# Attention with relative positions on one core: scores and value products merged in twos, PSUM ring cut from five banks to three

## The reference

```python
qkv = x @ qkv_w.T + qkv_b                     # x is the normed input; q and v also get x @ la.T @ lb.T
attn = einsum('bqd,bkd->bqk', q * hd ** -0.5, k)
rel_h = einsum('bhwc,hkc->bhwk', r_q, Rh)     # r_q is q as a 14 x 14 grid
rel_w = einsum('bhwc,wkc->bhwk', r_q, Rw)
attn = softmax(attn + rel_h[..., :, None] + rel_w[..., None, :])
out = (attn @ v) @ proj_w.T + proj_b          # output: input + out
```

## Time and profile before

| | us |
|---|---|
| median of 3 runs (3370.44 to 3375.27) | 3372.74 |
| the profiled execution, its own time | 3373.03 |
| its span | 3371.3 |
| TensorE matmuls busy | 3297.2 (98%) |
| DVE busy | 2528.2 (75%) |
| ACT busy | 2098.2 (62%) |
| share of the last chain of work on TensorE | 94% |
| mean granted TensorE clock | 0.991 |

### The profile page before, as it was taken

The page is one execution under the profiler, slowest core; times in us unless marked ns, Lnnn a source line. Parts: engine busy times, 40 slices in busy tenths (PEclk is TensorE's granted clock), DMA queues, the critical chain, the costliest instruction groups (busy, mean ns, idle before and its releaser), DMA issues.

```text
span 3371.3 us, 80148 instructions
## 1 busy us (share of the span) xinstructions
PE 3297.2 (98%) x31984; PEld 2130.7 (63%) x31984; DVE 2528.2 (75%) x5970; ACT 2098.2 (62%) x5651; POOL 35.8 (1%) x65
## 2 busy tenths in 40 slices
PE   7689999999999999999999999999999999999998
PEld 4456666666666666666666666666666666666665
DVE  7577777777777777777777777777777777777764
ACT  2466666666666666666666666666666666666664
POOL 0000000000000000000000000000000000000000
PEclk9799999999999999999999999999999999999999
DMA  3145664555555556565555555555565555565554
GB/s 128 42 96 109 120 122 103 115 113 112 118 121 107 113 112 114 116 121 107 110 116 113 112 123 118 101 117 111 110 127 120 100 118 108 111 126 122 103 106 105
DMA packets 1091412, 376.13 MB, mean 112 GB/s; under 512 B 916696, under 2 KB 1071320, under 8 KB 1091040
## 3 DMA queue, kind: packets, MB, share of 16 engines
q1 hardware_dynamic: 1075206, 333.63, 49.8%
q10 hardware_dynamic: 15834, 37.37, 3.9%
HBM read 86.60 MB, written 38.54 MB: 37 GB/s over the span
## 4 chain that ended last, share of the span: by engine, by line
PE 94%; DVE 2%; ACT 1%; issue 0%; DMA 0%; POOL 0%; SPq 0%; POOLq 0%; DVEq 0%
PE ring L556 51%; PE ring L623 17%; PE score L599 9%; PE o_ps L613 7%; PE ring L578 3%; PE ring L637 3%; PE ring L629 3%; ACT prob L682 1%; PE ring L642 0%; PE ring L563 0%; DVE split L789 0%; DVE row_max L769 0%; DVE rel_sb L762 0%; DVE split L781 0%; DVE rel_sb L756 0%
## 5 line engine op out<-in xcount | busy, mean ns | idle before, releaser
L556 PE MATMUL ring<-xn_hi,w_hi 128*128 128x392 f16 x3456 | 1143.2, 331 | 4.8 <-DVE xn_lo L839 4.6
L556 PE MATMUL ring<-xn_lo,w_hi 128*128 128x392 f16 x3456 | 1139.8, 330 | 0.0
L556 PE MATMUL ring<-xn_hi,w_lo 128*128 128x392 f16 x3456 | 1139.3, 330 | 0.5 <-issue 0.5
L682 ACT ACTIVATE prob<-score,neg_max,exp_scale 98x196 f32<-98x196 f32 x1536 | 769.8, 511 | 252.9 <-DVE neg_max L773 245.4
L769 DVE TENSOR_REDUCE row_max<-score 98x4 f32<-98x784 f32 x384 | 373.3, 972 | 273.2 <-PE score L599 272.1
L789 DVE SCALAR_TENSOR_TENSOR split<-prob,row_inv,split 98x196 f16<-98x196 f32 x1536 | 545.0, 417 | 7.8
L556 PEld LDWEIGHTS ring<-xn_hi,w_hi 128*128 128x128 f16 x3456 | 342.3, 99 | 260.7 <-issue 7.7
L556 PEld LDWEIGHTS ring<-xn_hi,w_lo 128*128 128x128 f16 x3456 | 338.8, 98 | 237.9 <-issue 3.6
L556 PEld LDWEIGHTS ring<-xn_lo,w_hi 128*128 128x128 f16 x3456 | 338.9, 98 | 208.3 <-issue 1.9
L623 PE MATMUL ring<-o_hi,w_hi 128*128 128x392 f16 x1152 | 380.2, 330 | 1.4 <-DVE o_lo L798 1.4
L623 PE MATMUL ring<-o_lo,w_hi 128*128 128x392 f16 x1152 | 379.8, 330 | 0.0
(11 more groups left out here) (118 smaller groups left out, 4896.7 us busy)
## 6 DMA issues: line engine op xcount, KB each, us to landing
y_sb<-in_x SPq DMA_DIRECT2D x192, 196.0 KB
out<-y_sb SPq DMA_DIRECT2D x192, 196.0 KB
x_sb<-in_x ACTq DMA_DIRECT2D x31, 1176.0 KB
rel_q<-rel_sb SPq DMA_DIRECT2D x128, 122.5 KB, 2.4
stage<-in_L_conv_qkv_w SPq DMA_DIRECT2D x3, 2304.0 KB, 15.4
turned<-split SPq DMA_TRANSPOSE x384, 4.2
rel_q<-rel_sb SPq DMA_DIRECT2D x128, 24.5 KB, 1.9
v_tok<-v_split SPq DMA_TRANSPOSE x192, 3.4
```

The lines of the kernel that those rows point to most:

```text
L556: last = T.matmul(ring[:, bank, 0:NT], w[:, c, 128 * j:128 * j + 128], xx[:, par, c, :], start=(c == 0 and part == 0), stop=(c == CT - 1 a ...
L682: last = A.activation(prob[:, head, half, :], score[0:HALF, head, TOK * half:TOK * half + TOK], ACT.Exp, bias=neg_max[:, k % 2, i:i + 1], ...
```

## The change

Each head pair's two scoring slots are issued in a row, and its two value slots too. For this the score tensor has four banks (image x head) and the ring three; prob has a half per image, S of slot k waits only for the exps of slot k - 2, and the four orders are rewritten. y_sb has two slots in place of three. The R tables keep one set of 32 columns per row in place of two.

```diff
-BANKS = 5
+BANKS = 3
-YS = 3
+YS = 2
 PE_ORDER = (
-    each("S", 0, 0) + each("P", 1, 10) + each("Z", 2, 5) + each("X", -1, 3, 4, 5) + each("V", 0, 0)
-    + each("S", 0, 1) + each("P", 1, 11) + each("K", 0, 1) + each("Y", 1, 0) + each("G", -1, 0)
-    + each("S", 0, 2) + each("P", 0, 0) + each("G", -1, 1) + each("V", 0, 1) + each("Y", 1, 1) + each("Z", 1, 0)
-    + each("S", 0, 3) + each("P", 0, 1) + each("K", 0, 2) + each("Y", 1, 2) + each("Z", 1, 1)
...
-    + each("S", 0, 9) + each("P", 0, 7) + each("R", -1, 0) + each("K", 0, 5) + each("R", -1, 1) + each("Y", 1, 3)
-    + each("S", 0, 10) + each("P", 0, 8) + each("R", -1, 2, 3, 4) + each("V", 0, 5) + each("Y", 1, 4) + each("Z", 1, 3)
-    + each("S", 0, 11) + each("P", 0, 9) + each("K", -1, 0) + each("X", -2, 0, 1, 2) + each("Y", 1, 5) + each("Z", 1, 4))
+    each("S", 0, 0, 1) + each("P", 1, 10, 11) + each("Z", 2, 5) + each("X", -1, 3, 4, 5) + each("V", 0, 0)
+    + each("K", 0, 1) + each("Y", 1, 0) + each("G", -1, 0)
+    + each("S", 0, 2, 3) + each("P", 0, 0, 1) + each("G", -1, 1) + each("V", 0, 1) + each("Y", 1, 1) + each("Z", 1, 0)
+    + each("K", 0, 2) + each("Y", 1, 2) + each("Z", 1, 1)
+    + each("S", 0, 4, 5) + each("P", 0, 2, 3) + each("V", 0, 2) + each("Z", 1, 2) + each("Q", -1, 0) + each("K", 0, 3)
+    + each("Q", -1, 1)
+    + each("S", 0, 6, 7) + each("P", 0, 4, 5) + each("V", 0, 3) + each("Q", -1, 2) + each("K", 0, 4) + each("Q", -1, 3, 4)
+    + each("S", 0, 8, 9) + each("P", 0, 6, 7) + each("Q", -1, 5) + each("V", 0, 4) + each("R", -1, 0) + each("K", 0, 5)
+    + each("R", -1, 1) + each("Y", 1, 3)
+    + each("S", 0, 10, 11) + each("P", 0, 8, 9) + each("R", -1, 2) + each("V", 0, 5) + each("R", -1, 3) + each("Y", 1, 4)
+    + each("R", -1, 4) + each("Z", 1, 3) + each("K", -1, 0) + each("X", -2, 0, 1) + each("Y", 1, 5) + each("X", -2, 2)
+    + each("Z", 1, 4))
 ACT_ORDER = (
...
+    each("Y", 2, 5) + each("N", 0, 0) + each("X", -1, 3) + each("T", 0, 0) + each("P", 1, 11) + each("X", -1, 4)
+    + each("N", 0, 1) + each("X", -1, 5) + each("V", 0, 0) + each("T", 0, 1) + each("K", 0, 1)
+    + each("Y", 1, 0) + soft(2) + each("P", 0, 1) + each("N", 0, 3) + each("V", 0, 1) + each("T", 0, 3)
+    + each("H", -1, 0) + each("Y", 1, 1) + each("K", 0, 2) + each("H", -1, 1)
+    + each("Y", 1, 2) + each("H", -1, 2) + soft(4) + each("P", 0, 3) + each("N", 0, 5) + each("V", 0, 2) + each("T", 0, 5)
...
+    + each("Y", 1, 3) + each("N", 0, 10) + each("R", -1, 2) + each("T", 0, 10) + each("V", 0, 5) + each("P", 0, 9)
+    + each("N", 0, 11) + each("R", -1, 3) + each("T", 0, 11) + each("Y", 1, 4) + each("R", -1, 4) + each("K", -1, 0)
     + each("X", -2, 0, 1, 2))
 DVE_ORDER = (
...
+    each("Z", 2, 4) + each("S", 0, 0, 1) + each("Z", 2, 5) + each("N", 0, 0) + each("X", -1, 3) + each("T", 0, 0)
+    + each("P", 1, 11) + each("N", 0, 1) + each("V", 0, 0) + each("T", 0, 1) + each("K", 0, 1) + each("X", -1, 4, 5)
+    + each("M", -1, 0)
+    + each("G", -1, 0) + each("S", 0, 2, 3) + each("G", -1, 1) + soft(2) + each("P", 0, 1) + each("N", 0, 3)
+    + each("V", 0, 1) + each("T", 0, 3) + each("H", -1, 0) + each("Z", 1, 0) + each("K", 0, 2) + each("H", -1, 1, 2)
+    + each("Z", 1, 1) + each("S", 0, 4, 5) + each("L", -1, 0, 1) + each("N", 0, 4) + each("L", -1, 2) + each("P", 0, 3)
+    + each("T", 0, 4) + each("V", 0, 2) + soft(5) + each("Z", 1, 2) + each("Q", -1, 0) + each("K", 0, 3)
...
+    + each("S", 0, 10, 11) + each("N", 0, 10) + each("R", -1, 2) + each("T", 0, 10) + each("V", 0, 5) + each("P", 0, 9)
+    + each("N", 0, 11) + each("R", -1, 3) + each("T", 0, 11) + each("R", -1, 4) + each("Z", 1, 3) + each("K", -1, 0)
     + each("X", -2, 0, 1, 2))
 SP_ORDER = (
...
+    each("ST", 2, 4) + each("CB", 0, 0) + each("LY", 1, 0) + each("ST", 2, 5) + each("T", 0, 0) + each("VT", 0, 0)
+    + each("T", 0, 1)
...
+    + each("T", 0, 10) + each("VT", 0, 5) + each("T", 0, 11) + each("CA", -1, 0) + each("ST", 1, 3) + each("LY", 1, 5))
...
-        rt_hi = sb(keep, "rt_hi", [128, 2, H, 64], F16)
+        rt_hi = sb(keep, "rt_hi", [128, 2, H, 32], F16)
...
-        prob = S("prob", [HALF, 2, 2, TOK], F32)
+        prob = S("prob", [HALF, 2, 2, 2, TOK], F32)
...
-        score = own.enter_context(nc.psum_tensor("score", [128, 2, 512], F32))
+        score = own.enter_context(nc.psum_tensor("score", [128, 2, 2, 512], F32))
...
-                    wait(sp, y_out[k % YS], 32 * p + 16 * (k // YS))
+                    wait(sp, y_out[k % YS], 16 * (CT // YS) * p + 16 * (k // YS))
...
-                                    last = T.matmul(cols, tab[rows, ax, row, 32 * head:32 * head + 32], mov,
+                                    last = T.matmul(cols, tab[rows, ax, row, :], mov,
...
-                    wait(pe, exps_done, 12 * p + k)
+                    wait(pe, exps_done, 12 * p + k - 1)
...
-                                last = T.matmul(score[0:HALF, head, to], stat[rows, qs], kk[rows, :],
+                                last = T.matmul(score[0:HALF, image, head, to], stat[rows, qs], kk[rows, :],
```

More of the change, by code:

```diff
@@ L76 @@
 ACT_ORDER = (
[L77 to L83, removed]
@@ new lines @@
+    + each("N", 0, 1) + each("X", -1, 5) + each("V", 0, 0) + each("T", 0, 1) + each("K", 0, 1)
+    + each("Y", 1, 0) + soft(2) + each("P", 0, 1) + each("N", 0, 3) + each("V", 0, 1) + each("T", 0, 3)
+    + each("H", -1, 0) + each("Y", 1, 1) + each("K", 0, 2) + each("H", -1, 1)
+    + each("Y", 1, 2) + each("H", -1, 2) + soft(4) + each("P", 0, 3) + each("N", 0, 5) + each("V", 0, 2) + each("T", 0, 5)
+    + each("Q", -1, 0) + each("K", 0, 3)
+    + each("Q", -1, 1) + soft(6) + each("P", 0, 5) + each("N", 0, 7) + each("V", 0, 3) + each("T", 0, 7) + each("Q", -1, 2)
@@ L90 @@
+    + each("LD", -2, 0) + each("K", 0, 4) + each("Q", -1, 3)
+    + each("Q", -1, 4) + soft(8) + each("P", 0, 7) + each("Q", -1, 5) + each("N", 0, 9) + each("V", 0, 4) + each("R", -1, 0)
+    + each("T", 0, 9) + each("K", 0, 5) + each("R", -1, 1)
+    + each("Y", 1, 3) + each("N", 0, 10) + each("R", -1, 2) + each("T", 0, 10) + each("V", 0, 5) + each("P", 0, 9)
+    + each("N", 0, 11) + each("R", -1, 3) + each("T", 0, 11) + each("Y", 1, 4) + each("R", -1, 4) + each("K", -1, 0)
     + each("X", -2, 0, 1, 2))
@@ L93 @@
 DVE_ORDER = (
[L94 to L106, removed]
@@ new lines @@
+    + each("M", -1, 0)
[3 more added lines that the diff above has]
+    + each("T", 0, 4) + each("V", 0, 2) + soft(5) + each("Z", 1, 2) + each("Q", -1, 0) + each("K", 0, 3)
+    + each("S", 0, 6, 7) + each("Q", -1, 1) + each("N", 0, 6) + each("T", 0, 6) + each("P", 0, 5) + each("V", 0, 3)
@@ new lines @@
+    + soft(7) + each("Q", -1, 2) + each("K", 0, 4) + each("Q", -1, 3)
+    + each("S", 0, 8, 9) + each("Q", -1, 4) + soft(8) + each("P", 0, 7) + each("Q", -1, 5) + each("N", 0, 9)
+    + each("V", 0, 4) + each("R", -1, 0) + each("T", 0, 9) + each("K", 0, 5) + each("R", -1, 1)
+    + each("S", 0, 10, 11) + each("N", 0, 10) + each("R", -1, 2) + each("T", 0, 10) + each("V", 0, 5) + each("P", 0, 9)
+    + each("N", 0, 11) + each("R", -1, 3) + each("T", 0, 11) + each("R", -1, 4) + each("Z", 1, 3) + each("K", -1, 0)
@@ L117 @@
 SP_ORDER = (
[L118 to L129, removed]
+    each("ST", 2, 4) + each("CB", 0, 0) + each("LY", 1, 0) + each("ST", 2, 5) + each("T", 0, 0) + each("VT", 0, 0)
+    + each("T", 0, 1)
+    + each("LY", 1, 1) + each("T", 0, 2) + each("VT", 0, 1) + each("T", 0, 3) + each("ST", 1, 0)
+    + each("ST", 1, 1) + each("LY", 1, 2) + each("T", 0, 4) + each("VT", 0, 2) + each("T", 0, 5) + each("ST", 1, 2)
+    + each("LY", 1, 3)
+    + each("T", 0, 6) + each("VT", 0, 3) + each("T", 0, 7) + each("LY", 1, 4)
+    + each("T", 0, 8) + each("VT", 0, 4) + each("T", 0, 9)
+    + each("T", 0, 10) + each("VT", 0, 5) + each("T", 0, 11) + each("CA", -1, 0) + each("ST", 1, 3) + each("LY", 1, 5))
 PER_PAIR = {"Q": 6, "K": 6, "V": 6, "R": RCH, "Y": 6, "Z": 6, "X": 6, "G": 2}
@@ L162, in build @@
         w_lo = sb(keep, "w_lo", [128, CT, 4 * C], F16)
-        rt_hi = sb(keep, "rt_hi", [128, 2, H, 64], F16)
-        rt_lo = sb(keep, "rt_lo", [128, 2, H, 64], F16)
+        rt_hi = sb(keep, "rt_hi", [128, 2, H, 32], F16)
+        rt_lo = sb(keep, "rt_lo", [128, 2, H, 32], F16)
         onehot = sb(keep, "onehot", [128, TOK], F16)
@@ L380, in _ @@
                 for head in range(2):
-                    for at in (32 * head, 32 * head + 16):
+                    for at in (0, 16):
                         rows = slice(64 * head, 64 * head + 64)
@@ L534, in _ @@
                 elif kind == "LY":
-                    wait(sp, y_out[k % YS], 32 * p + 16 * (k // YS))
+                    wait(sp, y_out[k % YS], 16 * (CT // YS) * p + 16 * (k // YS))
                     sp.dma_start(y_sb[:, k % YS], x_rows[p][:, :, 128 * k:128 * k + 128]).then_inc(y_in[k % YS], 16)
             for slot in range(YS):
-                sp.wait_ge(y_out[slot], 16 * 2 * pairs)
+                sp.wait_ge(y_out[slot], 16 * (CT // YS) * pairs)
         @block.tensor
```

(12 more changed lines are left out.)

15 lines of the change are left out of this document (removed).

## The result

The changed kernel takes 3441.2 us (median of 4 runs, 3438.9 to 3442.8) against 3372.2 before: a ratio of 1.020 (95% interval 1.0185 to 1.0221), 69 us slower. The forecast was 3416, range 3375 to 3460, slower with a chance of 0.80.

What follows compares the result with a forecast made beforehand. The prediction took TensorE's work, practically without waits, to bound the kernel. From 3373.0 us it took 71 for merged slots and added 114 for ring waits with three banks: 3416 us, range 3375 to 3460.

Steps and rivals of the forecast that it cites:

- What the change removes: Six merges of scoring and value slots per pair of images save 0.37 us each, 0.10 of it full-tiling return; 71 us.
- What costs nothing: Second score buffer, prob halves, smaller R tables, shorter memsets, moved X2 and two y buffers: all taken as 0.
- The rel copies as next bound: On SP, relative-position copies land late for the next pair's first scores, hidden only by the last group's waits; 0.7 us.
- The walk: Group by group, TensorE waits for both readers of the ring user three places earlier; 3.68 us per pair, 114 us.
- Groups b to f: Second to last merged groups of a pair of images; waits 0.51 in b, 0.54 in c, none d/e, 1.75 and 0.43 in f.
- the 1.75 us at Z3: In the last group, Z3 takes R3's bank and waits 1.75 us for ACT and DVE to read it.
- group a: First merged group of a pair of images, slots 0 and 1; one wait of 0.45 us forecast.
- The 0.45 at V0: In group a, V0 comes three ring places behind X3 and waits 0.45 us for ACT's late copy of it.
- 31 pairs times one value: Waits of 3.68 us counted for 31 pairs of images, since first and last have other neighbours; 114 us.
- The faster one: Rival: readers keep up, mainly at Z3 behind R3, so waits total under 2.2 us per pair; 3324 or 3302 us; chance 0.14.
- The clock: Rival: the granted clock falls behind each 1.75 us wait, adding up to 53 us; 3469 us; chance 0.12.
- The transposes' rival: Slot 1's transposed split lands 1 us late, so P1 waits in every pair; 31 us more, 3447 us; chance 0.10.

Runs made afterwards that it cites:

- Experiments 1: Changed kernel with TensorE's order inside all six merged groups set back to score, value, score, value; 3473.3 us, ratio 1.030 to the kernel before.
- 7: Kernel of experiment 6 with TensorE's order score, value, score, value inside each group; 3387.2 us, ratio 1.003 to the kernel before.
- experiment 4: Changed kernel with three y_sb slots in place of two, orders unchanged; 3437.0 us, ratio 1.019 to the kernel before.
- experiment 3: Changed kernel with ACT and DVE reading R3 before slot 11's softmax and P9, and ACT reading Y4 earlier; 3416.0 us, ratio 1.013 to the kernel before.
- experiment 8: Kernel of experiment 6 with SP issuing transpose T11 ahead of store ST3 and ACT loading the next input later; 3345.7 us, ratio 0.992 to the kernel before.
- experiment 6: Changed kernel with reader orders rewritten against ring waits, Y5 between X0 and X1, three y_sb slots, merge kept; 3351.9 us, ratio 0.993 to the kernel before.
- experiment 2: Kernel before the change with four ring banks instead of five and nothing else changed; 3577.9 us, ratio 1.061 to the kernel before.

## Why the prediction was right, and where it was off

*What bounds the kernel.* Right: TensorE's work, without slack. Experiments 1 and 7 show that this work counts where no wait covers it.

*What the change removes* (0.37 us per merge). Right in its pieces: 1.48 and 1.13 are 0.27 less than 2 x 0.81 and 2 x 0.63. The 0.10 of the return was not tested by itself, but the full 0.36 is gone from groups d and e. What I did not see is that part of the saving is worth nothing where a group ends in a wait anyway: undoing the merge costs 1.03 us per pair, not 1.6.

*What costs nothing.* Mostly right. Two y slots cost at most a few microseconds (4, unclear as a time, experiment 4). The rel copies as next bound were right (experiment 3).

*The walk.* Groups b to f came out within 0.1 us each, the 1.75 us at Z3 among them. The term of the sum that was mis-sized is group a, 0.45 us forecast and 0.75 measured. The 0.45 at V0 came out in size but mostly at another place, and this is partly luck: the X step ahead of it, X5, takes the bank of Z5, which DVE reads only behind slot 1's row maximum. The four matmuls of X5 take 0.79 us and 0.04 of idle (at 1688.56 in the chain above), where two X steps take 1.05; that is 0.30, and V0 and K1 lose another 0.17 (6.14 us, 5.97 in experiment 8). The rest is G0, for which the sum had no term: DVE reached the statistics late, since V0 and K1 had been delayed before it, and TensorE lost 0.27 us (0.04 of idle and 0.35 for a piece that is 0.12 in the kernels of 6 and 8, as in a pair before). Over 30 pairs the usual pair's net miss, 1.73 for 1.46 us, is 8 of the missing 26. The period of 102.2 us that I gave was met to 0.1 us by luck too: I had started from one pair of 100.7, where the usual one takes 100.47, and the two errors cancel.

*Single late pairs.* Another 8 us are pairs longer than the usual one, which the sum had put at nothing: a transposed tile that takes 10.4 us instead of 4.0, a row chunk that Z5 waits for.

*31 pairs times one value.* I let the first and the last pair count together as one. Of the forecast 43 us, 30 usual pairs at 1.46 take 43.8, which leaves -0.7 for the two ends, and they lost 9.4: this is the remaining 10, and the largest part. Part of it, by my estimate 3 us, is clock. From the first pair's S0 to the second's (after, then before; the same columns as in experiment 2):

```profile
145.10:247.70 102.60, 85.59 (x838) 56.47 (x837) 74.02 (x180) 60.49 (x169) 0.69 (x1) 0.89 0.46 88
144.60:239.20 94.60, 83.54 (x839) 54.03 (x840) 69.89 (x167) 59.09 (x167) 0.69 (x1) 0.93 0.44 89
```

The mean granted clock is 0.89 where it was 0.93, and TensorE is busy 2.1 us more, though six merges should save 1.6 by their pieces. Experiment 4, with the same orders, has 0.92 there and reaches the second pair's S0 2.3 us earlier. The rest I put down to the readers' chains, now of two slots in a row, being longer than the matmul work of a pair without neighbours; that was argued from the trace. Experiment 6 shows that other orders give back 7 of the 8.6, with a clock of 0.95 there.

*The rivals.* The faster one is refuted by Z3's wait in 30 of 30 pairs. The clock did not fall behind these waits: it is 1.00 in the stretches after the one at 1675 us, and 0.99 in the mean, as before. It did fall behind those of 4.4 us in experiment 2, and cost 1.4 to 2.4 us more each time, and it fell more than before in the first pair. The stated range says that it takes in most of this rival, but the rival's own figure, 3469, lies above its end of 3460; nothing here hangs on that. The transposes' rival was right in kind, but small and in few pairs: 5.1 us in 8 waits instead of 31 us in every pair. The advice of the Trainium skill (Perfetto Trace Analysis, section Matmul Optimizations) to keep all eight banks in play, taken alone, would have said 3302: all eight are in play in both kernels, and the loss lay in how few of them the ring had.

## What to carry to other kernels

Before banks are moved from one use to another, walk each user of the poorer ring: when has the slower of its two readers finished, in the order in which that reader's queue is written, and how much matmul work lies between? With a short ring the order of the readers matters more than their busy share: the same work with other reader orders, and a third y_sb slot that was worth about 4 us at most by itself, gave 89 us back, and only then did the gain from fewer changes of tiling show. Look at every wait that is hidden by the one you remove.

## What the hardware showed that I had not expected

- A scoring step (tiles of 64 rows) takes 0.81 us behind another kind of step and 0.67 behind its like, a value step (tiles of 64 columns) 0.63 and 0.50: a change of tiling, with the fill, is 0.14 and 0.13 us. The saved changes show in full in the pieces of the chain (1.48 and 1.13 us).
- A TensorE wait of 4.4 us, once per pair, lowers the granted clock each time and makes the next 18 matmuls take 4.58 to 5.60 us instead of 3.16. The 30 waits of 1.75 us at Z3 did not, though an idle of 1.8 us near the end of the kernel before did: the length of an idle alone does not say whether the clock falls.
- Transposing DMAs land 4.0 us after issue in the median and 10.4 at worst. With the 1.2 MB load of the next input issued two steps later on ACT, the outliers of the step that waits for the tile issued beside it were gone, and the worst landing was 6.6 us, against 10.2 in experiment 6 (one execution of each).
